# Reordering weight, vector and node-part loads around the first layer of a four-layer graph network

## The reference

```python
edge_feat = concat([x[src], x[dst], edge_attr])        # per edge
h = mish(edge_feat @ W1 + b1)
messages = mish(h @ W2 + b2)
agg = segment_sum(messages, dst)                       # per node
u = mish(concat([x, agg]) @ W3 + b3)
out = u @ W4 + b4
y = x + out;  x = layernorm(x + layernorm(y) * gamma + beta)
```

## Time and profile before

| | |
|---|---|
| median of the runs | 1333.17 us (1332.1, 1333.17, 1335.42) |
| profiled execution | 1339.57 us |
| its span | 1337.9 us, mean granted TensorE clock 0.970 |
| TensorE busy | 1249.6 us (93%) |
| DVE, ScalarE, POOL busy | 1021.2 (76%), 852.5 (64%), 673.8 us (50%) |
| edges' drain, last DMA of it issued | 873.3 |
| first layer's block | from 880.5 |
| count stage | 880.5 to about 944 |

### The profile page before, as it was taken

One profiled execution on the slowest core, in us unless ns is written; L12 is line 12 of the kernel. 1 busy time (PEld: TensorE's weight loads), 2 busy tenths in 40 slices (PEclk: granted clock), 3 DMA queues, 4 the chain that ended last, 5 costly groups with the idle time before them and its releaser, 6 DMA issues. The chain is left out here.

```text
span 1337.9 us, 18961 instructions
## 1 busy us (share of the span) xinstructions
PE 1249.6 (93%) x5844; PEld 1000.6 (75%) x5844; DVE 1021.2 (76%) x1799; ACT 852.5 (64%) x772; POOL 673.8 (50%) x484
## 2 busy tenths in 40 slices
PE   6976999999999999999999999958799996999998
PEld 5764777777777777777777777746687785888886
DVE  3425899999999999999999999735776247847444
ACT  3305999999999999999999999637633011312310
POOL 0136788888888887778887887117030000011000
PEclk8996999999999999999999999978999997999999
DMA  9987877778777777777777787668200510000001
GB/s 310 327 286 158 162 140 146 149 155 163 152 152 153 152 155 156 149 147 145 152 155 150 153 156 138 179 248 317 92 8 0 205 48 28 17 1 2 0 19 61
DMA packets 108315, 183.59 MB, mean 137 GB/s; under 512 B 35154, under 2 KB 44672, under 8 KB 108248
## 3 DMA queue, kind: packets, MB, share of 16 engines
q0 software_dynamic: 71056, 106.45, 41.3%
q1 hardware_dynamic: 30104, 64.09, 14.0%
q10 hardware_dynamic: 7088, 12.20, 2.7%
HBM read 141.21 MB, written 41.30 MB: 136 GB/s over the span
## 5 line engine op out<-in xcount | busy, mean ns | idle before, releaser
L220 POOL DMA_INDIRECT w_raw<-q_dram,idx_all x172 | 341.5, 1986 | 79.4 <-issue 56.2
L1041 PE MATMUL ps_x<-wA_hi,hT_hi 128*128 128x512 f32 x668 | 270.7, 405 | 1.5 <-DVE hT_lo L733 1.3
L1041 PE MATMUL ps_x<-wA_hi,hT_lo 128*128 128x512 f32 x668 | 264.4, 396 | 0.0
L1041 PE MATMUL ps_x<-wA_lo,hT_hi 128*128 128x512 f32 x668 | 264.0, 395 | 0.0
L220 POOL DMA_INDIRECT w_raw<-p_dram,idx_all x176 | 177.3, 1007 | 142.4 <-issue 109.8
L1041 PEld LDWEIGHTS ps_x<-wA_hi,hT_hi 128*128 128x128 f32 x668 | 125.6, 188 | 34.3 <-issue 2.0
L1041 PEld LDWEIGHTS ps_x<-wA_hi,hT_lo 128*128 128x128 f32 x668 | 125.5, 188 | 30.2
L1041 PEld LDWEIGHTS ps_x<-wA_lo,hT_hi 128*128 128x128 f32 x668 | 125.5, 188 | 28.3
L740 DVE TENSOR_TENSOR x<-ps_x,b 128x512 f32<-128x512 f32 x167 | 114.1, 683 | 25.4 <-PE ps_x L1041 18.4
L1675 POOL TENSOR_TENSOR tmp_n<-X,gam 128x512 f32<-128x512 f32 x10 | 13.9, 1392 | 227.0 <-DVE t_be L1760 182.4
L1000 PE MATMUL ps_x<-ident,w_raw 128*128 128x128 f32 x672 | 103.6, 278 | 14.3 <-DVE h L726 7.6
(11 more groups left out here) (270 smaller groups left out, 2876.7 us busy)
## 6 DMA issues: line engine op xcount, KB each, us to landing
ea_raw<-in_eaT SPq DMA_DIRECT2D x88, 128.0 KB
adj_dram<-adj_sb POOLq DMA_DIRECT2D x42, 210.2 KB
adj_dram<-agg_sb ACTq DMA_DIRECT2D x11, 640.5 KB
U_lo<-adj_dram SPq DMA_DIRECT2D x10, 640.0 KB, 8.6
adjT_dram<-adjT_sb SPq DMA_DIRECT2D x10, 640.0 KB, 7.9
adjT_rest<-adjT_dram SPq DMA_DIRECT2D x7, 640.0 KB, 9.6
w_raw<-in_w SPq DMA_DIRECT2D x4, 1024.0 KB, 11.7
w_raw_g<-in_w SPq DMA_DIRECT2D x4, 1024.0 KB, 7.8
```

Source lines behind the costliest of these rows:

```text
L220: g.indirect_dma_start(G[:, slot, c * D:(c + 1) * D], None, rows, bass.IndirectOffsetOnAxis(ap=idx_all[:, i:i + 1], axis=0), **op).then_in ...
L1041: last = t.matmul(ps_x2[c % 2][:, :], h[:, b.slot, e], w[:, k, :], start=(k == 0 and i == 0), stop=(k == KD - 1 and i == 2))
```

## The change

SP loads node parts 6 and 7 in the edge phase, behind the two weight loads, once the low parts of h1 are done (the memory of Y6 and Y7). In the first layer, the four node-part loads and three vector loads in front of tile 4 go; node parts 8 and 9 and four vectors (b_l among them now, which POOL used to load) are issued behind the counts of tile 9, in front of the store of tile 5. POOL asks for W_l as soon as W3's second half is split, waits for the four vectors, asks for W_r once W4 is split, and then does the subtraction and the ten adds. DVE waits for the four vectors in place of three and b_l.

```diff
@@ edge_phase, sync
                 sp.dma_start(raw[0], by_slices(w04)).then_inc(w4_in, 16)
+                sp.wait_ge(lo_ready, n * (NB * 2))
+                for r in range(ZE, 2 * KD):
+                    sp.dma_start(Z[r][:, :], z0_dram[(r - ZE) * P:(r - ZE + 1) * P, :]).then_inc(z_in[r - ZE], 16)
@@ first_layer, sync
                 for s in range(-SLOTS, R):
-                    if s == 0:
-                        for r in range(ZE, R):
-                            sp.dma_start(Z[r][:, :], z0_dram[(r - ZE) * P:(r - ZE + 1) * P, :]).then_inc(z_in[r - ZE], 16)
-                        for t, b in ((b4, b04), (gam, g0), (bet, be0)):
-                            sp.dma_start(t[:, :], bcast(b)).then_inc(vec_in, 16)
                     r = s + SLOTS
...
                         sp.dma_start(adj_in[:, r % SLOTS, :], adj_dram[r * P:(r + 1) * P, 0:NP]).then_inc(a_in[r % SLOTS], 16)
+                    if r == R - 1:
+                        for i in range(2 * KD, R):
+                            sp.dma_start(Z[i][:, :], z0_dram[(i - ZE) * P:(i - ZE + 1) * P, :]).then_inc(z_in[i - ZE], 16)
+                        for t, b in ((b4, b04), (gam, g0), (bet, be0), (bl, b1l)):
+                            sp.dma_start(t[:, :], bcast(b)).then_inc(vec_in, 16)
@@ first_layer, gpsimd
-                wait(vec_in, 48)
+                wait(w3_lo, KD)
+                g.dma_start(raw[1], by_slices(w1l)).then_inc(wl_in, 16)
+                wait(vec_in, 64)
+                wait(w4_lo, KD)
+                g.dma_start(raw[0], by_slices(w1r)).then_inc(wr_in, 16)
                 g.tensor_tensor(bet[:, :], bet[:, :], b4[:, :], ALU.subtract).then_inc(b_diff, 1)
                 for r in range(R):
                     g.tensor_tensor(X[:, cols(r)], X[:, cols(r)], b4[:, :], ALU.add).then_inc(xb_ready, 1)
-                wait(w3_lo, KD)
-                g.dma_start(raw[1], by_slices(w1l)).then_inc(wl_in, 16)
-                g.dma_start(bl[:, :], bcast(b1l)).then_inc(bl_in, 16)
-                wait(w4_lo, KD)
-                g.dma_start(raw[0], by_slices(w1r)).then_inc(wr_in, 16)
                 wait(xb_ready, R)
@@ first_layer, vector
-                dve_.wait_ge(vec_in, 48)
-                dve_.wait_ge(bl_in, 16)
+                dve_.wait_ge(vec_in, 64)
```

More of the change, by code:

```diff
@@ L168, in gnn @@
         w3b_in, w4_in, vec_in, zero_out = (sem(n) for n in ("w3b_in", "w4_in", "vec_in", "zero_out"))
+        z_in = [sem(f"n0_z_in{r}") for r in range(ZE, R)]
         p_in = [[sem(f"edge_p_in{i}{c}") for c in range(TE)] for i in range(2)]
@@ L201, in gnn @@
                        h1, Y, w_raw, b3, wA_hi, wA_lo, w3_hi, w3_lo, wc_hi, wc_lo, b2, agg_sb, p_dram, q_dram, agg_dram, adj_dram, eaT, xT_dram,
-                       w03, w04, w3b_in, w4_in, zero_out, p_in, q_in, ea_raw, ea_in)
+                       w03, w04, w3b_in, w4_in, zero_out, p_in, q_in, ea_raw, ea_in, z0_dram, z_in)
         Y += [sb(f"Y{r}", [P, D]) for r in range(2 * KD, R)]
@@ L210, in gnn @@
         first_layer(nc, sb, pb, sem, edge_sems, ident, half_pi, eps_col, X, U_hi, U_lo, Y, w_raw, w_hi, w_lo, b3, b4, gam, bet, deg, rdeg, nrdeg, has, slow,
-                    agg_dram, adj_dram, adjT_dram, z0_dram, w1l, b1l, w1r, w3b_in, w4_in, vec_in, adjT_held, adj_held, b04, g0, be0)
+                    agg_dram, adj_dram, adjT_dram, z0_dram, w1l, b1l, w1r, w3b_in, w4_in, vec_in, z_in, adjT_held, adj_held, b04, g0, be0)
         edge_numbers.close()
@@ L531, in edge_phase @@
                h1, Z, w_raw, b3, w2_hi, w2_lo, w3_hi, w3_lo, wc_hi, wc_lo, b2, agg_sb, p_dram, q_dram, agg_dram, adj_dram, eaT, xT_dram,
-               w03, w04, w3b_in, w4_in, zero_out, p_in, q_in, ea_raw, ea_in):
+               w03, w04, w3b_in, w4_in, zero_out, p_in, q_in, ea_raw, ea_in, z0_dram, z_in):
     HB = 2 * BE
@@ L1109, in first_layer @@
 def first_layer(nc, sb, pb, sem, sems_to_clear, ident, half_pi, eps_col, X, U_hi, U_lo, Z, w_raw, w_hi, w_lo, b3, b4, gam, bet, deg, rdeg, nrdeg, has, slow,
-                agg_dram, adj_dram, adjT_dram, z0_dram, w1l, b1l, w1r, w3b_in, w4_in, vec_in, adjT_held, adj_held, b04, g0, be0):
+                agg_dram, adj_dram, adjT_dram, z0_dram, w1l, b1l, w1r, w3b_in, w4_in, vec_in, z_in, adjT_held, adj_held, b04, g0, be0):
     with ExitStack() as ctx:
@@ L1137, in first_layer @@
             "aT_out", "st_ready", "mv_ready", "sd_ready", "rs_ready"))
-        z_in = [sem(f"n0_z_in{r}") for r in range(ZE, R)]
         row_in, a_in = [sem(f"n0_row_in{r}") for r in range(R)], [sem(f"n0_a_in{u}") for u in range(SLOTS)]
-        (wl_in, wr_in, bl_in, w3_hi, w3_lo, w4_hi, w4_lo, wl_hi, wl_lo, wr_hi, wr_lo, T_ready, hi_ready, lo_ready, z_out, z_ready, sig, atan, t_ready, aT_ready, aT_evac, d_ready,
+        (wl_in, wr_in, w3_hi, w3_lo, w4_hi, w4_lo, wl_hi, wl_lo, wr_hi, wr_lo, T_ready, hi_ready, lo_ready, z_out, z_ready, sig, atan, t_ready, aT_ready, aT_evac, d_ready,
          c_dve, deg_tr, b_diff, us_ready, xb_ready, xe_ready, u_T, u_hi, u_lo, y_ready, y_used, sc_ready, res_ready, co_ready, x_new,
@@ L1143, in first_layer @@
             sem("n0_" + n) for n in (
-                "wl_in", "wr_in", "bl_in", "w3_hi", "w3_lo", "w4_hi", "w4_lo", "wl_hi", "wl_lo",
+                "wl_in", "wr_in", "w3_hi", "w3_lo", "w4_hi", "w4_lo", "wl_hi", "wl_lo",
                 "wr_hi", "wr_lo", "T_ready", "hi_ready", "lo_ready",
```

## The result

The median is 1342.41 us after (6 runs, 1340.31 to 1343.2) against 1334.3 before (6 runs, 1331.2 to 1338.28): ratio 1.0062, interval 1.0048 to 1.0076. The change costs 8.1 us, between 6.4 and 10.1. The forecast was 1335.0 with a range up to 1340, and the measured time lies above it. The profiled execution after took 1343.2 us, its span 1341.5.

A forecast was written before the change was run, and what follows sets the result against it. The first layer's count stage was taken to bound the kernel. Drain +0.4, earlier turn of u_0 -1.15 and restart +2.55 summed to +1.8 us on 1333.17, giving 1335.0; the 8-in-10 range was 1329 to 1340.

The forecast's parts named there:

- The drain part: Two node-part loads at the edges' end: between 0 and +1.35 us, taken as +0.4.
- Tile 2's copy: ScalarE's copy of tile 2's turned counts, held by a store: predicted at 900.8, 2.0 us earlier.
- the turn of u_0: TensorE's turn of POOL's first u product: predicted at about 939.6, 1.15 us earlier than before.
- turn of u_2: TensorE's turn behind the first y product: predicted at 948.6 instead of 947.16, without the drain's 0.4.
- landing of the vectors: Vectors issued behind tile 9's counts, on which POOL waits: predicted landed at 922.9 from bytes at 389 GB/s.
- restart behind the wait for POOL: TensorE's slow clock after about 8 us idle before the turn of u_0: charged +2.55 us.
- the restart at tile 2: TensorE's slow clock behind tile 2's hole: taken as avoided, 2.55 us, with 2.0 from bytes 4.5 us.
- rival B: Vectors land late, at 926, through slower bytes or tile 2's restart: +4.9 us, 1338; chance 0.25.
- tile 7's copy: ScalarE's copy of tile 7's turned counts: predicted at 924.4 instead of 932.58, 8.2 us earlier.
- the 9.6 us that the working offered: Count stage alone: turn of u_0 at 931.1 instead of 940.75, if it did not wait for POOL.
- POOL's last products: POOL's products reaching into the first two y steps, slowing DVE: 0.45 to 0.9 us, left out of the sum.
- the forecast's own mechanism: POOL's subtraction and ten adds stand behind the late vectors; first u product 14.7 us later, TensorE waits about 8 us.

The follow-up runs named there:

- e6: The kernel before with only node parts Z6 and Z7 loaded in the drain; 1332.89 us, ratio 0.9999 to before.
- e12: The changed kernel run again unchanged for a second profile; 1338.54 us, ratio 1.0043 to before.
- e11: The kernel before run again unchanged for a second profile; 1331.58 us, ratio 0.9993 to before.
- e2: The changed kernel with DVE's four W_l splits at tiles 3 to 6 instead of 6 to 9; 1340.5 us, ratio 1.0049 to before.
- e3: The changed kernel with POOL's first five u products in front of its wait for the vectors; 1342.47 us, ratio 1.0066 to before.
- e5: e3 with POOL waiting for each of its ten adds before the next; 1334.47 us, ratio 1.0010 to before.
- e4: The changed kernel with both u products first and W_l splits at tiles 3 to 6; 1332.01 us, ratio 0.9990 to before.
- e7: The changed kernel with vectors asked for before tile 4, W_l splits at tiles 3 to 6, W_r behind SP's last store; 1332.33 us, ratio 0.9994 to before.
- e9: The kernel before with Z6, Z7 in the drain, Z8, Z9 behind tile 9's counts, W_r behind SP's last store; 1328.13 us, ratio 0.9963 to before.
- e10: e9 with the three vectors asked for one tile later; 1332.51 us, ratio 0.9996 to before.

## Why the prediction was wrong

**What held.** The chain is decided ahead of the second layer. The drain part costs next to nothing: the block's first issue came at 880.78 against 880.51, +0.27 for a predicted +0.4, of which the edges' last store already has 0.21 (873.53 against 873.32); e6 shows no effect on the time. Tile 2's copy was released at 900.49 (predicted 900.8). POOL ran from the landing to its first u product in the time predicted: 943.04 - 926.95 = 16.1 us to the turn of u_0 (predicted 16.7). TensorE waited 6.68 us for it and came back at half the clock. What the turn of u_2 loses (953.02 against 947.16, 5.86 us) arrives at the second layer as 5.79.

**Where it failed: the landing of the vectors and the restart behind the wait for POOL, both sized too small, and a DVE term left at nothing.** The turn of u_2 was put at 948.6 within the layer, 949.0 with the drain's 0.4, and came at 953.02, 4.0 us later. Counted from 948.6 it is 4.4 us, in two terms:

- *Landing of the vectors, 922.9 predicted, 926.9 measured.* The last count load went out at 914.55 instead of 913.2 (+1.35), with the restart at tile 2, booked as avoided, paid: behind a hole of 1.92 us the turns took 2.25 us. The issues took 4.15 us (914.92 to 919.07) instead of 3.5 (+0.65). The rest, 1.9 us, is the time behind the last issue, 7.8 us instead of 5.9. This is rival B, to within a microsecond of its 926. The bytes were slower, too: 377 GB/s from 882 to 908 (windows above) where the earlier trace rows have 389. And the byte sum was short by a unit: a row's KB are 1024 bytes (640.0 KB for 128 x 1280 x 4) and its GB 10^9, so 14720 KB at 389 GB/s take 38.7 us and not 37.8. With the landing offset of `bet` worked out again in the same way (2.9 us instead of 3.2) the landing would have been put 0.7 us later. Less 0.6 for POOL's shorter chain, the turn of u_0 was 3.4 us late.
- *The restart behind the long hole, 2.55 predicted, 3.57 measured.* From the turn of u_0 to that of u_2 it is 953.02 - 943.04 = 9.98 us, against 6.41 in before. Of that, 0.44 is a wait for DVE's late low part; the rest is the clock, 0.50 from 942 to 947. In e12 the same stretch takes 948.35 - 938.92 = 9.43 us, 3.02 more than in before.

So on the first pair of profiles the sum is +5.8 where the prediction had +1.8. The forecast gave rival B a chance of 0.25 and 1338 us for this; B's mechanism is what happened, and its restart term was short. The time missed the forecast by 7.4 us (1342.41 against 1335.0): 4.0 are these terms, 1.1 is the median of before, which the forecast had from three runs (1333.17) and six put at 1334.3, and 2.3 are in no term.

The stage itself gained less than booked, too. TensorE was ready for the turn of u_0 at 943.04 - 6.68 = 936.4 and not at about 931, because tile 7's copy came at 927.78 and not at 924.4, behind a hole of 3.24 us with a slow restart (929.15 above). Of the 9.6 us that the working offered a u_0 in time, 4.4 were there (940.75 - 936.4).

**A gain that was not there to be had.** The working was made on one profile, and booked the stall at tile 2 (2.0 + 2.55 us) as removable. In e11 the slow restart at tile 2 does not exist; after had one (2.25 us for ten turns), and after again did not. In e11 the turn of u_0 comes 933.28 - 868.41 = 64.9 us behind the edges' last store, against 67.4 in the first profile (940.75 - 873.32), so the restart's 2.55 us were already saved in it, without the change. Measured from the edges' last store, the change costs 182.4 - 176.9 = 5.6 us on the first pair (rounded sums) and 181.2 - 174.3 = 6.9 us on the second. The medians differ by 8.1, interval 6.4 to 10.1; the second comparison has 1.0043, some 5.7 us. The 6.9 us lie within both intervals (the second is 2.7 to 8.9), the 5.6 just under the first. Outside this stretch the change costs nothing that shows: from the second layer's start to the end after takes 285.5 and 285.7 us (1337.4 - 1051.68, e12), before again 285.5.

**The path that was missed.** DVE's subtraction beside POOL's adds. The prediction looked for DVE and POOL in each other's way only at POOL's last products, priced it at 0.45 to 0.9 us and left it out of the sum. It asked which DVE work lies beside the products, but not which lies beside the adds, which the change moved from 900 to 929, onto W_l's splits. "SBUF — State Buffer" of the Trainium skill, section "SBUF: two separate sides", says that a VectorE instruction with two SBUF inputs and a GpSimd instruction that reads SBUF share a pair of ports, and that whichever starts first holds the pair for its whole instruction and the other waits. For one add of about 1.25 us in front of it that would have made 1.9 us of a subtraction of 0.68; the trace has 11.72, so the wait was for the train and not for one instruction, and the measurement decides. In after this path ends beside POOL's, 0.44 us behind it: taken away alone (e2) it gives nothing clear. It would have made the obvious repair of the forecast's own mechanism, e3, fail.

## What to carry to other kernels

A load is worth moving later only if the list of the engine that waits for it is later too: count what stands behind that wait in order (here bet, ten adds and a product, 16 us) against the slack of its reader. When a train of GpSimd operations moves, list the VectorE instructions with two SBUF operands that come to lie beside it, and leave gaps in the train or move them away (here 0.18 us behind each add gave back 8.0 us, e5 against e3, and the two-input work moved away 10.5, e4 against e3). Book a stall as a gain only if a second profile of the same program shows it; and where two paths end together, try their repairs jointly, since each alone shows nothing (1340.5 and 1342.47 against 1332.01 for both).

## What the runs showed of the hardware

- *A train of GpSimd adds without gaps can keep out a VectorE operation with two SBUF inputs until it ends:* 11.72, 11.69 and 12.64 us in after, e12 and e3, for an operation of 0.68 us; with gaps of 0.18 us 1.19 us (e5). It doesn't always: in before such subtractions ran beside the same ten adds in 0.70 and 1.04 us, and the adds then took 13.31 us instead of 12.32. DVE's timeline of before, and POOL's, cut to one add beside each:

```profile
905.11 0.70 DVE L1312 TENSOR_TENSOR wA_lo<-w_raw,wA_hi 128x512 fp32r<-128x512 f32 x1
...
908.95 1.04 DVE L1312 TENSOR_TENSOR wA_lo<-w_raw,wA_hi 128x512 fp32r<-128x512 f32 x1
```

```profile
905.22 1.73 POOL L1290 TENSOR_TENSOR X<-X,b 128x512 f32<-128x512 f32 x1
```

```profile
909.38 1.75 POOL L1290 TENSOR_TENSOR X<-X,b 128x512 f32<-128x512 f32 x1
```

The next add pays: 1.73 and 1.75 us instead of 1.25 to 1.3. The profiles of before, e6, e7, e9, e10 and e11 hold twelve such subtractions beside the ten adds, of 0.68 to 1.77 us, all begun in the fourth add or later; the three that were kept out began in the first add (930.13 in after, whose first add runs from 928.98 to 930.27). Whether that is the condition was not tested.
- *The length of a hole does not by itself say whether the clock falls.* Behind holes of 2.11 (e11), 2.46 (e9), 2.47 (e12) and 2.80 us (e5) ten turns took 1.28 us, at 2.4 GHz; behind 1.92 us (after) and 2.07 us (e4) 2.25 and 2.24 us, begun at 1.2 GHz. What was different before those holes was not tested.
- *Vectors spread over 128 rows (256 KB) in a loaded queue* took 6.6 to 7.9 us from issue to landing in after, 5.6 to 8.1 in e12. DMA issues of after, the first and the last of the four:

```profile
b<-in_b SPq DMA_DIRECT2D x1, 256.0 KB, 6.6
...
b<-in_b1l SPq DMA_DIRECT2D x1, 256.0 KB, 7.9
```

From 915 to 927 the DMA engines were busy all the time (share 1.01) and moved 347 GB/s, where the prediction reckoned with 389:

```profile
915.00:927.00 12.00, 10.29 (x59) 8.32 (x57) 6.06 (x7) 9.68 (x11) 0.05 (x1) 1.00 1.01 347
```
